# A two-layer decoder on one core: half of a state-space step moved into the attention, the first steps of each gated block moved ahead, and TensorE given matmuls nobody reads at eight seams

## The reference, cut to what matters

```
x = ln(x + linear_attention(x))                 # layer 0
x = ln(x + mixed(x, ctx))                       # causal self + cross attention, 16 heads of 16, then one projection
x = ln(x + experts(x))                          # 8 experts, each on 128 tokens of batches 0,1 and 128 of batches 2,3
x = ln(x + state_space(x))                      # layer 1: conv of 4 taps, in-projection, softplus, scan over tokens, out-projection
y = ln(x) * g + b
x = ln(x + block(y, y, causal) -> ln -> block(., ctx))
    block: softmax attention, 16 heads of 32, projection, + x,
           then gelu(ln(.) @ li2) @ li3, + x    # the "MLP" of each block
x = ln(x + scaled_ffn(x))                       # gated by silu, then two 1024 x 1024 layers
```

## Time and profile before

| | |
|---|---|
| median of three runs | 3734.82 us |
| the profiled execution, its own time | 3736.43 us |
| its span in the trace | 3735.2 us |
| TensorE busy, mean granted clock | 3284.9 us (88%), 0.943 |
| VectorE, ScalarE, GpSimd busy | 2270.9, 1664.5, 1050.5 us |

### The profile page before, as it was taken

How to read it: one execution, slowest core, us unless ns; L and a number is a source line. 1 busy time by engine, 2 the same in 40 slices (tenths; PEclk the granted TensorE clock), 3 DMA queues, 4 the chain that set the end, 5 groups by cost and what they waited for, 6 DMA issues and landing times. The chain is left out here.

```text
span 3735.2 us, 61586 instructions
## 1 busy us (share of the span) xinstructions
PE 3284.9 (88%) x22796; PEld 2124.6 (57%) x22796; DVE 2270.9 (61%) x4545; ACT 1664.5 (45%) x3072; POOL 1050.5 (28%) x1281
## 2 busy tenths in 40 slices
PE   6888999999988858989685999999999968899998
PEld 3554545545437745655473555555556537778787
DVE  6788787787943466655366766766766525433442
ACT  1136666566662313444431555455555644223222
POOL 1030120301210123443341555545455543000000
PEclk9989999999998978999896999999999989999999
DMA  2031222222214116554205435343344111222111
GB/s 73 1 74 45 68 52 67 54 47 70 55 25 155 67 42 84 84 81 71 72 32 68 70 48 74 49 62 60 59 61 64 32 41 57 74 64 85 59 60 57
DMA packets 144641, 229.59 MB, mean 61 GB/s; under 512 B 40916, under 2 KB 84696, under 8 KB 141400
## 3 DMA queue, kind: packets, MB, share of 16 engines
q1 hardware_dynamic: 129048, 216.21, 28.0%
q10 hardware_dynamic: 15296, 9.45, 1.0%
HBM read 99.39 MB, written 8.91 MB: 29 GB/s over the span
## 5 line engine op out<-in xcount | busy, mean ns | idle before, releaser
L1123 DVE TENSOR_REDUCE a_mp<-bank 128x1 f32<-128x384 f32 (+2 forms) x1280 | 684.2, 590 | 367.3 <-PE bank L972 366.6
L1079 ACT ACTIVATE a_p<-bank 128x512 f32<-128x512 f32 (+1 forms) x1088 | 586.6, 600 | 475.7 <-PE bank L1002 344.2
L1125 DVE TENSOR_REDUCE mx_mp<-bank 128x2 f32<-128x512 f32 (+2 forms) x1088 | 611.2, 621 | 104.2 <-PE bank L972 65.5
L1079 ACT ACTIVATE mx_p<-bank 128x512 f32<-128x512 f32 (+3 forms) x1088 | 524.1, 571 | 268.3 <-PE bank L1002 267.0
L1164 POOL TENSOR_TENSOR a_pair<-a_p 128x512 f32<-128x512 f32 x384 | 490.9, 1309 | 481.5 <-ACT a_p L1079 397.4
L1002 PE MATMUL bank<-a_qs,a_ks 128*128 128x512 f32 (+1 forms) x1088 | 461.1, 439 | 31.1 <-DVE a_mp L1123 12.7
L972 PE MATMUL bank<-a_ks,a_qs 126*128 126x384 f32 (+2 forms) x1280 | 450.4, 396 | 41.9 <-ACT a_v L2035 9.4
L276 POOL TENSOR_TENSOR rs<-ve,neghalf 128x4 f32<-128x4 f32 (+2 forms) x80 | 78.7, 984 | 1101.3 <-DVE ve L271 1057.7
L1002 PEld LDWEIGHTS bank<-a_qs,a_ks 128*128 128x128 f32 (+1 forms) x1088 | 199.4, 187 | 260.8 <-issue 164.4
L972 PEld LDWEIGHTS bank<-a_ks,a_qs 126*128 126x128 f32 x1280 | 247.4, 196 | 124.5 <-DVE a_mp L1123 30.0
L972 PEld LDWEIGHTS bank<-mx_ks,mx_qs 62*128 62x128 f32 x2176 | 180.3, 192 | 186.1 <-issue 133.7
(11 more groups left out here) (308 smaller groups left out, 5591.3 us busy)
## 6 DMA issues: line engine op xcount, KB each, us to landing
sf_raw<-in_h_w SPq DMA_DIRECT2D x64, 512.0 KB, 3.5
a_ks<-a_kh SPq DMA_DIRECT2D x96, 192.0 KB, 4.5
ex_w<-in_L_ffn_w SPq DMA_DIRECT2D x16, 1024.0 KB, 5.8
a_qs<-a_qh SPq DMA_DIRECT2D x64, 256.0 KB, 6.6
mx_ks<-mx_kh SPq DMA_DIRECT2D x192, 64.0 KB, 2.2
a_ks<-a_kl SPq DMA_DIRECT2D x48, 192.0 KB, 5.2
mx_qs<-mx_qh SPq DMA_DIRECT2D x128, 64.0 KB, 2.2
mx_rec<-mx_flat SPq DMA_DIRECT2D x128, 64.0 KB, 2.0
```

The source lines that it names most:

```text
L1079: act.activation(probs[place % len(probs)][0:kp, q0:T], self.bank(part, n, kb, h)[0:kp, q0:T], ACT.Exp, scale=scale).then_inc(*self.frees( ...
L1123: v.tensor_reduce(best[:, j:j + 1, i, s], bank[:, 0:w], AX.X, ALU.max).then_inc(*self.frees(part, n, *at, r))
L1125: v.tensor_reduce(best[:, r:HG:tiled, i, s], bank.rearrange("p (k c) -> p k c", k=HT)[:, :, 0:w], AX.X, ALU.max).then_inc(*self.frees(part ...
```

## The change

1. The state space's second half is no longer run after the experts. It is a chain of steps (`state_chain`) given to the planner of `a1`, which places its TensorE steps where a bank is free and the rest as their inputs come (`lazy` and `others`). Batches 1 and 2 swap places in `X` (`BATCH_IN`) so that each half is two neighbouring batches. It works in buffers that `a1` needs only later.
2. `mlp_lead`: the load and split of the first MLP weight, and the norm, turn and first four `f` parts of batch 0, go into the last jobs of the attention before; the four `f` parts stand behind its last totals. The MLP begins at `f` 4.
3. `keep_busy`: a run of bf16 matmuls of 256 columns into a free bank, at eight seams (counts doubled in the code: 56, 76, 52, 60, 32, 100, 28, 40).
4. In mixed attention the last batch's cross jobs go ahead of its self jobs, the cast of the maxima goes from VectorE to ScalarE, and three numbers of its policy change. Its planner now also counts the clearing of the slots.
5. Buffers are shared between stages (`store`), which is what makes room for 1 and 2; the bf16 identity is made in mixed attention; one key part of `a2` is 384 wide in place of 450.

```diff
+BATCH_IN = 0, 2, 1, 3
-MIXED = Policy(900, 900, 350, 400, -160, 140, -50, 350, 50, -40, 200, 200, 2.6, 4.5)
+MIXED = Policy(900, 900, 350, 350, -10, 140, -30, 350, 70, -40, 200, 200, 2.6, 4.5)
+STATE_FROM, STATE_APART = 0, 3.0
+LEAD = 4
+LEAD_AT = {False: ((6, "raw", 0), (9, "stats", 0), (11, "high", 0), (12, "low", 0), (13, "norm", 0), (14, "turn", 0), (14, "turn", 1)),
+           True: ((40, "raw", 0), (41, "stats", 0), (43, "high", 0), (44, "low", 0), (45, "norm", 0), (47, "turn", 0), (48, "turn", 1))}
+BUSY = dict(la=28, mx_y=38, mx=26, ex=30, a1=16, ma1=50, a2=14, ma2=20)
...
+    def keep_busy(self, place):
+        pe, bank = self.nc.tensor, min(self.banks, key=lambda bank: (bank in (bank.pool.held if bank.pool else ()), bank.takes))
+        pe.wait_ge(bank.freed.sem, bank.takes)
+        for _ in range(2 * BUSY[place]):
+            pe.matmul(bank.tile[:, 0:2 * P], self.ones[:, :].bitcast(BF16)[:, 0:P], self.ones[:, :].bitcast(BF16), start=True, stop=True)
...
+        lazy, others = ([step for step in chain if (step[2] in ("turn", "in", "proj")) == bank] for bank in (True, False))
...
+            able = [step for step in lazy if until(step) <= done]
+            if able and at >= STATE_FROM and side.idle and len(side.held) < 2:
+                yield start("full", max(side.next().back_at, *(ready[step] for step in until(able[0])))), policy.beside, lazy
...
-            elif part == "tops_turned" and not summed:
-                if n:
-                    v.wait_ge(*has(f"peak{(n - 1) % q_slots}", n - 1))
-                v.wait_ge(*self.full("turn_tops", n))
-                v.tensor_copy(turned[:, :], self.bank("turn_tops", n)[0:2 * HG, :]).then_inc(*self.frees("turn_tops", n))
...
-        jobs = [job(b, kind, 2 * pair + i) for b in range(NB) for kind in ("self", "cross") for pair in range(NG // 2) for i in range(2)]
+        jobs = [job(b, kind, 2 * pair + i) for b in range(NB) for kind in (("self", "cross") if b < NB - 1 else ("cross", "self")) for pair in range(NG // 2) for i in range(2)]
...
+                y_after=lambda: [self.full("residual", tag, b - len(ys), TB - 1)] if b >= len(ys) else
+                                [self.full("residual", "ss", 3, TB - 1)] if b and not cross else [],
...
+        state_chain = [] if cross else [("state", s, kind, i) for kind, ss, n in (
+            ("edges", 1, 1), ("turn", 2, KC), ("conv", 2, KC), ("residual", 2, 1), ("in", 1, 3), ("softplus", 1, 1), ("delta", 1, 1),
+            ("decay", 1, 1), ("scan", 1, 1), ("proj", 2, TB), ("stats", 2, 1), ("out", 2, 1), ("park", 2, 1)) for s in range(ss) for i in range(n)]
...
-            nc.vector.wait_ge(*self.freed("residual", tag, 0, TB - 1))
-            self.moments(lambda t: self.X[:, t, :], TB, "in", tag, 0)
-            self.rsqrt(TB, "in", tag, 0)
-            self.fence(("root", "in", tag, 0))
+            self.keep_busy(tag)
+            self.fence("parts_made", "mlp_f", ("weight_low", f"{tag}_li2_w"), ("filled", "mlp_x", 0, KC - 1), *(("filled", "mlp_f", 0, i) for i in range(LEAD)))
```

546 lines of the change are left out of this document (364 added, 182 removed).

## The result

The kernel after takes 3715.12 us (median of 4 runs, 3704.01 to 3718.92) against 3737.22 of the kernel before in the same comparison; ratio 0.9934, 95% interval 0.9919 to 0.9950. 22 us were gained; I had forecast 78, and a range that ended at 3698. The profiled execution of after took 3704.01 us (span 3702.8, mean granted clock 0.958), 32.4 less than that of before. It is the fastest of after's four, 11 us under their median, so 10 of these 32.4 us are not in the medians. The account by stages is made between these two; each length is the distance between two marked instructions. Exponentials are counted from the first: the 17th is the first of the second job.

The account below looks back on a forecast made before the run. TensorE was taken to bound the long attentions, with time to be had in the seams; 3736.4 - 42.2 + 10 - 30 + 3 - 14 - 3 = 3660, median 3659 us, range 3628 to 3698.

Parts of the forecast that it names:

- State space out: Between the last expert's norm and a1's first norm: moving the state space's second half away saves 42.2 us.
- State space in a1: Inside a1: the moved state-space work costs 10 us there, bounds 0 and 28.
- Sum: 12 - 4 + 3: a1's cost: 12 us push of the first maxima, 4 back from spread transfers, 3 for the out-projection; rounded to 10.
- the 450 that I had named as a sign of being wrong: a1 from norm to last totals: forecast 434 us; over 450 us would show the prediction wrong.
- 3 (the out-projection) behind it: Behind a1's start, where TensorE is the bound: the state space's out-projection costs 3 us of TensorE at full clock.
- The other 13 us of VectorE: In a1: VectorE's remaining state-space work falls into 45 us with 25 busy, hidden at no cost; up to 13 otherwise.
- Rival B: State space in a1: handovers hold the in-order queues, all VectorE work is paid, +30 for +10, 3679 us; chance 0.14.
- Leads: MLP starts: first gelu 15.4 us earlier in each, taken as -30, with 3 us cost in the attentions' last jobs.
- Unread matmuls: At the seams: runs of matmuls nobody reads hold TensorE's clock, worth 14 us, bounds 0 and 18.
- Shared buffers: Buffers shared between stages: the same instructions in other places, 0 us.
- Mixed attention: Mixed attention: reordered last jobs and 32 casts leaving VectorE give -3 us, bounds -17 and +8.
- rival D: Mixed attention: the maxima's cast waits in ScalarE's queue, delaying 32 jobs; 3755 us at 3 us a job; chance 0.05.

Follow-up runs that it names:

- e_alone: The changed kernel with the state space's second half run alone ahead of a1's first steps, nothing of it beside the attention; 3721.62 us, 0.9954 to before.
- e_banks: The changed kernel, its planner also noting when the bank of each state-space out-projection step comes back; 3702.46 us, 0.9916 to before.
- e_late: The changed kernel with the MLPs' lead behind the attention's last adds instead of in its last jobs; 3754.38 us, 1.0039 to before.
- e_early: The changed kernel with batch 2's input steps in a1 at their old place, 4 blocks earlier; 3714.02 us, 0.9931 to before.
- the note on all steps: The changed kernel, its planner noting when the bank of every step beside an attention comes back, in all three attentions; 3638.61 us, 0.9741 to before.
- e_nobusy: The changed kernel without any of the 416 matmuls nobody reads; 3720.96 us, 0.9950 to before.
- e_long: The changed kernel with longer runs of unread matmuls ahead of a1, a2 and MLP 1 (92, 136, 64 for 60, 100, 32); 3710.19 us, 0.9921 to before.
- e_place: The changed kernel with 224 bytes of padding a partition ahead of the scaled layer's gate weights; 3708.83 us, 0.9911 to before.
- e_mixed: The changed kernel with mixed attention's old job order, cast of the maxima on VectorE and old policy numbers; 3726.50 us, 0.9965 to before.
- e_align: The changed kernel with 32 bytes of padding a partition ahead of three groups of buffers (a1's, both MLPs', gate weights); 3715.22 us, 0.9934 to before.

## Why the prediction was wrong

**State space out: right.** -41.4 for -42.2.

**State space in a1: wrong, the step that failed.** "Sum: 12 - 4 + 3, rounded down to 10 ... Bounds: 0 ... and 28". `e_alone` measures 31.2, outside the bounds, and a1 from its norm to its last totals took 465 us, over the 450 that I had named as a sign of being wrong. I had priced work. The part ahead of the first exponential was about right (6.6 us, for 12 less 4). Two terms behind it were not. For the out-projection I had "3 (the out-projection) behind it", 16 matmuls by their length: it took 13.9 us, a circle of matmul, add, bank, and `e_banks` took 9.8 off a1's first 17 exponentials with the work unchanged. And "The other 13 us of VectorE ... hidden, at nothing" counted VectorE's free time over 45 us, not what waits in the queue behind them: the second job's maxima, which came 37.4 us behind the first's in place of 10.6. With the circle gone 18.1 us of the 27.9 remain there. That part is read from the traces; no run moved VectorE's share by itself. The trace of before had no such circle, but it had the like: searches that waited for the adds of `mx_xb`, 7.7 us in 12 waits. I read "TensorE 839 of 900 us busy" as full, and never asked what the other 61 us waited for. Rival B (30 us for a chain whose handovers hold the queues) had the right size in a1; its 3679 and the misses in a2 and the scaled layer make 3701. I gave it 0.14.

The remaining 10 us of a1 are in no term of mine. Neither lead (`e_late`: 0.7) nor the later place of batch 2's steps (`e_early`: none) explains them. With the note on all steps a1's last part went from 286.9 to 270.4, below before, by other banks alone; so the likeliest cause is how banks fell in the new order. That is not shown: before has the fault too, and no run compares the two orders without it.

**Leads: right.** -15.0 and -15.2 for -15.4 each. Their cost of 3 us was 10.5 in these traces (`e_late`), nearly all of it in a2, where the spread allows 5 to 10; I had counted only TensorE's turns and a delayed exponential.

**Unread matmuls: less than half came.** 4 to 6 us for 14. "One to three us of idle time stay between a run and the work it is for" was too kind: 4.07, 3.92 and 3.60 stayed at three seams (2.9, 2.9 and 1.8 us not gained). The seams with 1.25 and 1.54 are 4.4 and 2.4 us shorter than in before for 3.6 and 2.9, but that is in part luck. At mixed attention's projection the run is worth 0.8: without it (`e_nobusy`) the first two groups took 3.40 and 1.99 us, where before had 3.78 twice; in after they take 1.99 twice. Ahead of mixed attention it is worth 3.2 (29.5 to 26.3, turn to first reduction), yet before had 26.95 there, so something else in the new start costs 2.6, and the rest of the 2.4 lies ahead of the turn, where traces of the same instructions differ by 5. `e_long` closed the gap at a1 and got 2.3 there.

I had set a rule of the Trainium skill beside this ("TensorE: Matmul & The Clock Gate", Part 4: PE-mode transpose), by which turns don't count as work and the clock would be lost in them again. The trace does not bear that out here: in `e_long` eight turns of 1.06 us and 2.67 us of idle time stand between the unread matmuls and a projection at full clock (1.97). The idle gaps alone don't settle it either. At the last seam, stretches of TensorE in after (length, busy, clock, DMA share, GB/s):

```profile
3157.00:3160.00 3.00, 1.16 (x9) 0.86 0.67 228
3160.00:3164.00 4.00, 4.00 (x10) 0.50 1.01 378
```

Turns at full clock and a gap of 1.80, and then half. What is different there was not tested.

**Shared buffers: wrong.** "Shared buffers ... the same instructions in other places, 0" left out that a place has a price: +9.7 us in the scaled layer, shown by `e_place` (535.1 for 545.7).

**Mixed attention: right in sign, too small.** -13.4 for -3 in this pair. Of it 7.4 lie ahead of the first exponential, from none of the three edits that I had in mind (`e_mixed` keeps them), and what made them was not tested; the 6.0 behind it do not stand clear of the spread (866.8 and 870.6 before, 864.2 to 868.8 after). Cast and policy are worth 10 to 15 us in the changed kernel, but before, without them, was no slower than 866.8 to 870.6. My slower rival D, the cast that delays each job by ScalarE's queue, did not come about.

In all, measured less forecast in the profiled pair, the spread included: a1 +32.7 (41.3 for 8.6), a2 +8.0 (6.6 for -1.4), scaled layer +13.7 (9.7 for -4.0), mixed attention -10.4, the rest +4.7; that is 48.7, the distance from -81.1 to -32.4.

## What to carry to other kernels

An engine that is 93% busy still has the other 7% to explain: list what ends its waits, and where a wait is for a result that the instruction doesn't read, it is a buffer's return and the planner's choice of buffer that costs. Work that is moved beside other work must be priced by its longest circle (matmul, add, bank back), and by what stands behind it in each queue (here the next job's maxima), not by its sum. And after buffers are shared or moved, compare one matmul's length in a stage that the change doesn't touch.

## What the hardware showed

- A back-to-back matmul of 512 columns (128x128 weights, fp32r, full clock) took 0.2267, 0.2289 or 0.2333 us by where its operands lie in memory. It was 0.2267 where both start alike modulo 1,024 bytes: all at 928 in before, all at 896 in `e_place`. It was 0.2333 in after, with one operand at 896 and the other at 672. Alike modulo 64 is not enough: in `e_align` it was 0.2333 with the moving operand at 896 and the weights at 704, and 0.2289 with the two the other way round. Which distance decides stays open; over about 1,900 matmuls it is 10 us. The Trainium skill ("SBUF — State Buffer", Who interferes with whom) gives a matmul's moving operand and its weight load ports of their own; by that the operands' places would not matter to each other, and the measurement differs.
- Behind a run of unread bf16 matmuls that ended 0.58 us ahead of a1's turn, turn and projection took 1.06 and 1.97 us, at full clock; behind a gap of 4.07 us, 1.94 and 3.75, at half. With gaps of 0.58 to 1.54 us the work next behind was at full clock at every seam shown here, with 3.6 to 4.1 us none was wholly so. At the last seam the clock was lost behind the turns, at a gap of 1.80.
- With some 0.6 us of idle time ahead of each pair of 256-column matmuls the granted clock fell to half in the out-projection of after: 0.70 us a pair became 1.19 from the fourth on. With the same pairs back to back (`e_banks`) it stayed full. The gaps are the likely reason; nothing else was varied.
- One bank taken again at once costs the whole way round, a pair of matmuls, the add and the bank's return: 1.3 us a step at full clock and 1.8 at half in the out-projection of after. Eight such steps took 13.9 us, and 4.9 on other banks.
